# A graph layer and a mixture of experts on one core: TensorE given products that nobody reads, in the waits of the expert assignment

## What is computed

```
h   = relu(sage(layernorm(x), edges, W_self0, W_neigh0, b0))
x   = x + sage(h, edges, W_self1, W_neigh1, b1)
t   = layernorm(x)                                  # 1250 x 1024
lg  = silu(t @ rw1 + rb1) @ rw2 + rb2               # 1250 x 8, the router
idx = top_k(lg, 2); w = softmax over the two values
eh  = silu(t @ ew1[e] + eb1[e])                     # 1024 -> 256, expert e
eo  = eh @ ew2[e] + eb2[e]                          # 256 -> 1024
out = x + (t + sum over the two chosen experts of w * eo)
```

## Time and profile before

| | |
|---|---|
| median of three executions | 1129.91 us |
| profiled execution, its own time | 1135.2 us |
| its span | 1133.0 us |
| TensorE busy | 1060.1 us, 94% |
| VectorE, ScalarE, GpSimd busy | 54%, 38%, 16% |
| mean granted clock of TensorE | 0.968 |

### The profile page before, as it was taken

The page is one execution under the profiler, slowest core; times in us unless marked ns, Lnnn a source line. Parts: engine busy times, 40 slices in busy tenths (PEclk is TensorE's granted clock), DMA queues, the critical chain, the costliest instruction groups (busy, mean ns, idle before and its releaser), DMA issues.

```text
span 1133.0 us, 17970 instructions
## 1 busy us (share of the span) xinstructions
PE 1060.1 (94%) x6444; PEld 1011.8 (89%) x6444; DVE 616.1 (54%) x1093; ACT 428.2 (38%) x934; POOL 185.3 (16%) x194
## 2 busy tenths in 40 slices
PE   4999999999989999999998999999999299999992
PEld 3999999999989999999998999999999199999892
DVE  6678888888652343235222523363221767888672
ACT  5555444453311312121122012263322366767661
POOL 5500000000000011001100110004450215444332
PEclk9999999999989999999999999999999569999996
DMA  7332133212217650033103320385554269999965
GB/s 192 88 101 71 46 102 106 92 49 73 97 42 237 189 153 1 1 99 103 29 1 106 96 51 1 98 261 156 164 156 168 99 255 324 301 350 298 294 118 90
DMA packets 72793, 148.86 MB, mean 131 GB/s; under 512 B 11867, under 2 KB 50712, under 8 KB 68210
## 3 DMA queue, kind: packets, MB, share of 16 engines
q1 hardware_dynamic: 61041, 112.50, 30.9%
q0 software_dynamic: 10976, 34.65, 12.5%
q10 hardware_dynamic: 672, 0.32, 0.1%
HBM read 108.40 MB, written 42.96 MB: 134 GB/s over the span
## 4 chain that ended last, share of the span: by engine, by line
PE 73%; DMA 12%; issue 5%; DVE 5%; PEld 2%; POOL 1%; DVEq 1%; ACT 1%; POOLq 0%; ACTq 0%; PEldq 0%
PE ps L1464 20%; PE ps L941 14%; DMA out<-o_rows,to_i 11%; PE ps L1536 10%; PE ps L1503 9%; PE ps L1195 8%; PE ps L813 4%; PE ps L2098 2%; PEld ps L737 2%; POOL out L2050 1%; PE ps L2119 1%; PE ps L909 1%; PE ps L2084 1%; DVE key_hot L806 1%; PE ps L1522 1%
## 5 line engine op out<-in xcount | busy, mean ns | idle before, releaser
L1426 POOL TENSOR_TENSOR s_rows<-s_rows,b1t 125x1368 f32<-125x1368 f32 (+3 forms) x9 | 23.5, 2630 | 583.3 <-DMA s_rows<-in_x 583.3
L820 DVE TENSOR_TENSOR adj<-ps,adj 125x250 f32 x212 | 87.9, 415 | 41.8 <-PE ps L813 33.6
L941 PE MATMUL ps<-h_lo,w_hi 128*128 128x418 f32 x336 | 108.6, 372 | 0.0
L941 PE MATMUL ps<-h_hi,w_hi 128*128 128x418 f32 x336 | 100.2, 379 | 0.0
L1503 PE MATMUL ps<-z_lo,adj 125*125 125x342 f32 (+1 forms) x300 | 95.4, 323 | 2.7 <-issue 2.7
L1503 PE MATMUL ps<-z_hi,adj 125*125 125x342 f32 (+1 forms) x300 | 96.0, 325 | 2.0 <-DVE s_rows L1735 2.0
L941 PE MATMUL ps<-h_hi,w_lo 128*128 128x418 f32 x336 | 93.5, 359 | 0.0
L2187 DVE TENSOR_TENSOR w_lo<-w_raw,w_hi 128x2048 fp32r<-128x2048 f32 x34 | 77.9, 2290 | 28.3 <-ACT w_hi L2144 21.4
L1195 PE MATMUL ps<-adj,y_hi 125*128 125x416 f32 (+1 forms) x240 | 86.4, 360 | 3.4 <-issue 3.4
L1195 PE MATMUL ps<-adj,y_lo 125*128 125x416 f32 (+1 forms) x240 | 86.1, 359 | 0.7 <-issue 0.7
L813 PE MATMUL ps<-key_hot,src_hot 125*125 125x250 bf16 x424 | 80.8, 271 | 3.3 <-DVE adj L820 3.1
(11 more groups left out here) (304 smaller groups left out, 2655.8 us busy)
## 6 DMA issues: line engine op xcount, KB each, us to landing
w_raw<-in_L_ffn_ew SPq DMA_DIRECT2D x34, 1024.0 KB, 8.5
xin<-in_x SPq DMA_DIRECT2D x10, 448.0 KB
t_d<-xn SPq DMA_DIRECT2D x10, 448.0 KB
base<-x_d POOLq DMA_DIRECT2D x10, 448.0 KB, 4.2
out<-base POOLq DMA_DIRECT2D x10, 448.0 KB, 3.5
y_d<-y_hi SPq DMA_DIRECT2D x7, 625.0 KB
y_d<-y_lo SPq DMA_DIRECT2D x7, 625.0 KB
self_d<-self SPq DMA_DIRECT2D x7, 625.0 KB
```

The lines of the kernel that those rows point to most:

```text
L820: e.tensor_tensor(cols, ps[0:P, 5 + b % 2, 0:KW].rearrange("p (t w) -> p t w", t=NT), cols, ALU.add).then_inc(self.took, 1)
L941: mm = e.matmul(BANK(m, own, c), wt[:, own, k, :], ht[:, k, a:a + w], start=(k == 0 and p == 0), stop=(k == KT - 1 and p == 2))
L1426: e.tensor_tensor(cols, cols, b1t[:, 0:w].rearrange("p (a n) -> p a n", a=1).to_broadcast([P, n, w]), ALU.add).then_inc(s_x, 1)
```

## The change

A helper `keep_busy(e, times)` is added. It issues so many products of bf16 operands into bank 3: the stationary operand is `before_b`, the moving operand is the first column of `all_b`, repeated over 512 columns. Nothing reads the result. It is called at four places in TensorE's queue: 14 products ahead of the wait for `sel`, behind a new wait for `g_c` at 31; 30 behind line 1969; 12 behind line 1974; and 10 between groups 0 to 1 and groups 2 to 3 of step 0's `turn`.

```
+        def keep_busy(e, times):
+
+            for _ in range(times):
+                e.matmul(ps[0:P, 3, 0:512], before_b[:], all_b[:, 0:1].to_broadcast([P, 512]), start=True, stop=True)
+
         @on("tensor")
         def _(e):
+            e.wait_ge(g_c, 21 + NT)
+            keep_busy(e, 14)
             e.wait_ge(g_dve, 1)
...
             e.matmul(ps[0:P, 7, 0:NT * NX], counts[:], later_b[:], start=False, stop=True).then_inc(g_pe, 1)
+            keep_busy(e, 30)
             e.wait_ge(g_dve, 3)
...
             mm.then_inc(g_pe, 1)
-
+            keep_busy(e, 12)
...
-            turn(0, 0, 0)
+            turn(0, 0, 0, range(0, 2))
+            keep_busy(e, 10)
+            turn(0, 0, 0, range(2, 4))
             skewed(e, NS, head, tail)
```

## The result

The changed kernel takes 1139.23 us (median of 20 executions, 1130.33 to 1150.79), the kernel before 1129.9 us (20 executions, 1117.83 to 1147.28). The ratio is 1.0114, with a 95% interval of 1.0086 to 1.0141: slower. I had forecast 1129.0 with a range up to 1132.0.

What follows compares the result with a forecast made beforehand. TensorE at half clock from 907 to 923.6 us was taken as the bound, VectorE's chain before it. Turn 1 at 911.5 instead of 912.4 gave -0.9, from the median 1129.9 to 1129.0 us; range 1125.5 to 1132.0.

Steps and rivals of the forecast that it cites:

- The four places of products: Assignment: 14, 30, 12 and 10 products, 3.2, 6.9, 2.8 and 2.3 us at 2.4 GHz; only the 14 charged, +0.6.
- the two ends that I had named: Delay of `sel` by the 14 products: 0 if the clock never fell, +2.1 us if all run at 1.2 GHz.
- The 12: Products from 897.0 us: 2.8 us at 2.4 GHz, hidden before the rows at 900.63; at 1.2 GHz 4.9, +1.3.
- The rows of step 1 as the next to be late; the clock falling there: Behind head 0: rows come at 911.2 us, limiting the gain to 0.9; TensorE idles about 2 us, clock falls.
- nothing comes of it: Rival: clock falls between 903.5 and 907 us, before the head, which stays at 1.2 GHz; 1129.7, up to 1131; chance 0.22.
- the premise that the clock does not rise in the narrow step: From 907 to 923.6 us: once down, the clock stays at 1.2 GHz under unbroken narrow products until wide ones come.
- Nothing is removed or moved, 66 products are added.: TensorE's queue in the assignment: the change was costed as 66 products plus a wait on `g_c` that costs nothing.
- I let a gain or loss at 930 us pass through to the end one for one.: Behind step 0: transfers there wait for the compute, so time won or lost at 930 us reaches the end whole.
- The window with a DMA share of 0.01: Behind step 0: DMA engines' busy share of 0.01, taken to show that transfers there wait for the compute.
- Held throughout: Rival: full clock to 925 us, head 1 starts 2.1 us sooner, its first half saves 0.8; 1127.0 or 1125.5; chance 0.27.
- Slower: Rival: products hold up `sel`, the 14 starting at 1.2 GHz; +2.1, full case +8.7, 1138.6; half-way 1131 to 1132; chance 0.12.
- Swallowed: Rival: the gain at 930 us is levelled out by scatters landing on busy DMA engines; 1129.9, give or take 1; chance 0.07.

Runs made afterwards that it cites:

- after_again: The changed kernel once more, as a repeat; ratio 1.007 against the kernel before.
- after_third: The changed kernel a third time, beside later runs on the same chip; ratio 1.011 against the kernel before.
- before_again: The kernel before once more, unchanged, as a control; ratio 0.998.
- narrow_half: The changed kernel with its 66 products (14, 30, 12, 10) cut to 8 columns, run a second time; ratio 1.011 against the kernel before.
- narrow_whole: The changed kernel with 127 products of 8 columns (30, 62, 30, 5), 254 added instructions; ratio 1.001 against the kernel before.
- narrow: The changed kernel with its 66 products cut from 512 to 8 columns, same instructions in the same places; ratio 1.008 against the kernel before.
- end132: The kernel before with 132 semaphore increments behind TensorE's last product; ratio 0.999.
- hold_all: The changed kernel with 127 products of 304 columns (23, 50, 20, 27, and 7 ahead of head 0); ratio 0.996 against the kernel before.
- hold_5q: The changed kernel with 158 products of 240 columns (29, 62, 26, 33, 8), 316 added instructions; six executions, no ratio, median 1138.6 us beside 1132.4.
- hold_all_again: The changed kernel with 127 products of 304 columns, 7 of them ahead of head 0, run a second time; ratio 0.999 against the kernel before.
- late_head: The changed kernel with 28 more unread products behind step 0's last transposes, 188 added instructions; ratio 1.001 against the kernel before.
- narrow_3q: The changed kernel with 95 products of 8 columns (24, 44, 22, 5), 190 added instructions; ratio 1.008 against the kernel before.
- halves_again: The changed kernel with 127 products of 256 columns (26, 59, 24, 18), run a second time; ratio 1.002 against the kernel before.

## Why the prediction was wrong

- **The four places of products.** The price was right: 0.22 to 0.23 us each at 2.4 GHz. The first 14 put `sel` back by 0.8 us in the result's trace (forecast 0.6), by 2.2 in after_again (6.10 us, all at 1.2 GHz) and not at all in after_third: the two ends that I had named both came. The 12 were hidden in the first trace only; in the other two they took 4.47 and 4.27 us and left no idle time behind them.
- **The rows of step 1 as the next to be late; the clock falling there.** The number was right, the place of the fall was not. Turn 1 came 1.0 us earlier (forecast 0.9), with an idle time of 0.87 us ahead of it (forecast 1 to 2.5) and 0.50 behind. But the clock fell ahead of that wait, 2.5, 0.6 and 1.4 us into head 0 in the three traces (at 905.3, 909.1 and 901.7 us), and in the last two there is no idle time ahead of turn 1 at all. What stood ahead of each fall were the wait for `xt_lo` (1.1 to 1.5 us) and 0.98 us ahead of head 0, the thin stretch that I had given to "nothing comes of it". Head 0 took 3.06, 4.85 and 4.02 us, not 2.7. And the premise that the clock does not rise in the narrow step came from one trace: in before_again it rose at 915.9 us, in head 0.
- **"Nothing is removed or moved, 66 products are added."** This step failed. I costed the added instructions by the time that TensorE needs for them, and TensorE had that time. What I put at nothing is their number: instructions are themselves fetched by DMA, in a stage that keeps the DMA engines busy, and the count of those ahead decides where in the steps each fetch falls. Between narrow_half and narrow_whole it is worth 6 to 10 us. narrow shows that the loss needs no work in the products, end132 that it needs them ahead of the steps, narrow_whole that a whole piece more takes it away. That it is the fetch that does it is argued, from the period of one piece and the shifted places above; no run moves a fetch and nothing else.
- **"I let a gain or loss at 930 us pass through to the end one for one."** Wrong as well. Four profiled executions (before_again, end132, hold_all, narrow_whole) need 178 us from the first scatter to the last, the kernel before needed 186.9 in the execution that I read, and the changed kernel 189.6 to 190.3, whatever each had won ahead. In all eight traces with 132 to 188 added instructions TensorE waits 4.2 to 6.5 us in the middle of the steps and then has 13.7 to 17.1 us at 1.2 GHz; of the other twelve only those of hold_5q and hold_all_again show it. The window with a DMA share of 0.01 that I argued from was the last one of its kind: in the kernel before the share is 0.27 in the next 4 us and 1.02 from 934 to 1038 us. In the traces with the starved wait a landing, not the start, sets the pace.
- **The rivals.** "Held throughout" came about in the trace of late_head, whose clock is at 1.00 from 882 to 1035.7 us, and nearly in that of hold_all; neither shows the 2.9 us I gave it. "Slower" was given for the wrong place: its full case, 1138.6, is near the measured time, but the products that it charged with 8.7 us cost 0.8 us or, in after_again, about 2.5. "Swallowed" had no loss in it. No rival had a cost for the number of instructions, so the range ended at 1132.0. The 2% that I took for what a measurement can tell was too coarse; the intervals here are about 0.4% to either side.

Behind the starved wait stands a rule that I had read only for the assignment: the Trainium skill (TensorE: Matmul & The Clock Gate, HAM oscillation) says that a wait for data between bursts brings the clock down. The traces agree: after 5.35 us of waiting the clock was at 0.50 for 13.7 us, though TensorE was busy for 11.87 of them. A wait of 2.7 us in narrow_3q brought no fall.

**Open.** How a fetch of about 1 us makes a landing several us longer is not shown. That fetches start beside the long scatter and gather of narrow_half is seen in one trace; which DMA engine they share is in no record here. A run that moves the fetches without adding instructions ahead was not found. Why the executions of one and the same kernel spread over 2 to 3% (1117.83 to 1147.28 us before) is open too, and so is what the shortest have in common beyond the 178 us.

## What to carry to other kernels

Fillers on an idle engine are not free because their time is: here 132 instructions with hardly any work in them cost 0.5 to 1.1% (narrow and narrow_half) in a stage that keeps the DMA engines full, and 254 cost nothing. Test a filler against its twin with hardly any work and with another number of instructions before crediting or blaming the clock, and read a second trace of the kernel before: its own course varied by 2.7 us at the first tail. And where a stage is a loop of gathers and scatters with a share near 1, take a few us won at its start as unproven until the end shows them.

## What was not expected of the hardware

- TensorE's instruction pieces: 16 KB, every 11 to 28 us while the expert steps run, 0.88 to 2.01 us each. The starved wait of the changed kernel is not a wait for one: none starts between 1024.4 and 1047.5 us.
- A semaphore increment in TensorE's queue took 0.15 us (132 in 20.05 us), more than a product of 8 columns with its weights (0.11 us at 1.2 GHz, 62 in 6.75 in narrow_whole).
- Under unbroken narrow products the clock came back at very different times. In the first trace of the kernel before it stayed at 1.2 GHz from 907 to 922.3 us, where the wide ones begin; it rose behind 8.5 us of narrow products and transposes in before_again and behind 6.8 us in halves_again (window, length, and the columns of the earlier trace rows):

```profile
907.40:915.90 8.50, 8.50 (x41) 8.50 (x41) 3.22 (x3) 4.31 (x5) 1.80 (x2) 0.50 1.02 425
...
902.00:908.80 6.80, 6.80 (x35) 6.80 (x34) 1.22 (x1) 2.91 (x4) 1.58 (x2) 0.50 1.01 422
908.80:912.00 3.20, 3.20 (x30) 3.20 (x30) 3.20 (x4) 2.58 (x4) 0.00 (x0) 0.99 1.01 411
```
